# Graph network kernel: products of the first graph layer in the record stage, fixed memory map, graph layers written out from the last node tile

## What is computed

```python
for l in range(3):
    neigh = segment_sum(h[src], dst, n) * inv_deg
    h = h @ Ws_self[l] + neigh @ Ws_neigh[l] + bs[l]
    if l != 2: h = relu(h)
x1 = layernorm(x + h)
# second network, for every edge: e = mlp(edge_attr);
# e_new = mlp([e, mesh_nfeat[src], x1[dst]]) + e
# agg = segment_sum(e_new, dst); n_new = mlp([x1, agg]) + x1
out = layernorm(x1 + n_new)
```

## Time and profile before

| | us |
|---|---|
| runs | 2556.55, 2556.91, 2559.67 (median 2556.91) |
| profiled execution | 2557.4, its span 2555.7 |
| scatters (GpSimd) | from 30.8 to 294 of the span |
| counts (TensorE, VectorE) | from 299.5 to 421.6 |
| P0, S0 | from 431.0 to 492.7, from 497.8 to 550.7 |
| P1, S1 | from 550.9 to 610.5, from 614.0 to 670.1 |
| P2, S2 | from 670.3 to 729.8, from 733.3 to 806.3 |
| P3 | from 806.5 to 868.4 |
| stages c, d | from 876 to the end |

### The profile page before, as it was taken

One profiled execution on the slowest core, in us unless ns is written; L12 is line 12 of the kernel. 1 busy time (PEld: TensorE's weight loads), 2 busy tenths in 40 slices (PEclk: granted clock), 3 DMA queues, 4 the chain that ended last, 5 costly groups with the idle time before them and its releaser, 6 DMA issues. The chain is left out here.

```text
span 2555.7 us, 44732 instructions
## 1 busy us (share of the span) xinstructions
PE 2279.1 (89%) x13410; PEld 1928.7 (75%) x13413; DVE 1410.0 (55%) x3084; ACT 1170.4 (46%) x2117; POOL 1142.9 (45%) x1677
## 2 busy tenths in 40 slices
PE   2991288999988689999999999999999999999888
PEld 1430287777766578888888888888888888888776
DVE  7000297434344256666666666666666666666566
ACT  0210012232321156666666666666666666666521
POOL 4777400202020145555555555555555555555333
PEclk9996699999998889999999999999999999999989
DMA  6221001001012353233233233323232333323121
GB/s 184 78 68 19 14 0 37 11 27 37 1 36 75 101 145 63 60 61 63 59 64 59 63 60 62 62 57 66 57 65 58 62 61 59 64 59 64 30 89 42
DMA packets 76273, 149.57 MB, mean 59 GB/s; under 512 B 14690, under 2 KB 15790, under 8 KB 76220
## 3 DMA queue, kind: packets, MB, share of 16 engines
q0 software_dynamic: 44864, 93.18, 19.0%
q1 hardware_dynamic: 31243, 55.63, 6.6%
q10 hardware_dynamic: 112, 0.11, 0.0%
HBM read 129.12 MB, written 19.46 MB: 58 GB/s over the span
## 5 line engine op out<-in xcount | busy, mean ns | idle before, releaser
L1192 DVE CUSTOM_DVE_ANT_0 c_var_bank<-c_var_bank,c_p,k_floor 128x512 f32<-128x512 f32 x176 | 133.5, 758 | 369.6 <-PE c_var_bank L1349 369.6
L1083 POOL DMA_INDIRECT c_from_src<-s_dst_table,c_at_nodes x176 | 284.0, 1614 | 31.7 <-issue 31.7
L1403 PE MATMUL c_edge_bank<-c_m_hi,c_pt_hi 128*128 128x512 f32 x704 | 291.8, 414 | 0.0
L1404 PE MATMUL c_edge_bank<-c_m_lo,c_pt_hi 128*128 128x512 f32 x704 | 276.7, 393 | 0.0
L1405 PE MATMUL c_edge_bank<-c_m_hi,c_pt_lo 128*128 128x512 f32 x704 | 275.4, 391 | 0.0
L1077 POOL DMA_INDIRECT c_from_src<-s_mesh_table,c_at_nodes x176 | 206.4, 1173 | 150.7 <-POOL c_at_nodes L1073 141.9
L1089 POOL TENSOR_TENSOR c_dev<-c_var,k_half 128x1 f32<-128x1 f32 x176 | 98.1, 557 | 381.8 <-DVE c_var L1179 381.8
L1347 PE MATMUL c_var_bank<-c_m_hi,c_pt_hi 128*128 128x384 f32 x704 | 226.7, 322 | 4.7 <-ACT c_var_bank L1272 4.7
L263 POOL DMA_INDIRECT s_records<-a_stage_rec,a_stage_row x170 | 202.8, 1193 | 56.8 <-issue 48.7
L1347 PE MATMUL c_var_bank<-c_m_hi,c_ht_hi 128*128 128x384 f32 x704 | 226.1, 321 | 0.0
L1298 ACT ACTIVATE c_h<-c_from_src 128x512 f32<-128x512 f32 x176 | 111.2, 632 | 248.5 <-DVE c_from_src L1211 248.5
(11 more groups left out here) (298 smaller groups left out, 6097.9 us busy)
## 6 DMA issues: line engine op xcount, KB each, us to landing
k_w<-in_L_gnn_Ws_self_dram SPq DMA_DIRECT2D x3, 1024.0 KB
k_w<-in_L_gnn_Ws_neigh_dram SPq DMA_DIRECT2D x3, 1024.0 KB
c_from_src<-s_mesh_table,c_at_nodes POOLq DMA_INDIRECT x176
c_from_src<-s_dst_table,c_at_nodes POOLq DMA_INDIRECT x176, 4.7
s_records<-a_stage_rec,a_stage_row POOLq DMA_INDIRECT x170
a_mesh<-in_L_gnn_mesh_nfeat_dram SPq DMA_DIRECT2D x10, 250.0 KB
k_h<-in_x_dram SPq DMA_DIRECT2D x1, 2500.0 KB
s_mesh_table<-a_mesh_out SPq DMA_DIRECT2D x10, 250.0 KB
```

Source lines behind the costliest of these rows:

```text
L1083: pool.indirect_dma_start(from_src[u][:], None, scratch["dst_table"], bass.IndirectOffsetOnAxis(ap=at_nodes[u][:, 1:2], axis=0), compute_o ...
L1192: dve.tensor_tensor_reduce(var1_bank[:], var1_bank[:], p[u % 2][:], 1.0 / D, k["floor"][:, 0:1], ALU.mult, ALU.add, var[u][:, 0:1]).then_i ...
L1403: pe.matmul(edge_bank[:], left[0], m_hi[1][:, c, :], start=False, stop=False, skip_group_check=True)
L1404: pe.matmul(edge_bank[:], left[0], m_lo[1][:, c, :], start=False, stop=False, skip_group_check=True)
```

## The change

1. **P0 moves into stage a.** TensorE makes the products of the first layer after the mesh tiles and ahead of the counts. ScalarE converts the two weight matrices and the first two tiles of `h` ahead of its mesh copies, VectorE writes `w_lo` after its second mesh copy. SyncE issues the bias, the next layer's weights and the next bias ahead of the read-back of the records.
2. **One memory map.** `Region` puts the tensors of both stages at fixed addresses, so that those of P0 outlive stage a. One-hot matrices now lie over the sort's temporaries. No instruction comes of this by itself.
3. **Stage b without loops**, from node tile 9 down to 0, so the S0 pass can begin when only `adj[9]` has been subtracted; each further subtraction is made one tile at a time during S0 (`own_counts`). The test whether the low parts of the counts are needed (`many`) comes at the start of stage b.
4. **TensorE waits for `a_hi`**, and for `a_lo` only inside the branch. The transpose for the next P pass moves from ahead of the last S tile to behind it.
5. **GpSimd splits the second layer's weights at the start of stage b** instead of after P0.
6. **In S2 SyncE loads `x` tile i+2 ahead of its wait for normalised tile i.**

The core of the diff:

```diff
+SORT_AT, TEMP_AT, FOLD_AT, SBUF_END = 87296, 112128, 132864, 229344
@@ phase_a, SyncE
+        sp.dma_start(bias0[:], rows(t["L0_gnn_bs"][0]).broadcast_to([NPB, D])).then_inc(bias_in, 16)
+        sp.wait_ge(w_lo_ok, 2)
+        sp.dma_start(w[0][:], chunked(t["L0_gnn_Ws_self"][1])).then_inc(w_next, 16)
+        sp.dma_start(w[1][:], chunked(t["L0_gnn_Ws_neigh"][1])).then_inc(w_next, 16)
+        sp.wait_ge(self_ok, NB)
+        sp.dma_start(bias0[:], rows(t["L0_gnn_bs"][1]).broadcast_to([NPB, D])).then_inc(bias_next, 16)
@@ phase_a, VectorE, between the second and third mesh copy
+        for i in range(2):
+            dve.wait_ge(w_hi_ok, i + 1)
+            dve.tensor_tensor(w_lo[i][:], w[i][:], w_hi[i][:].bitcast(F32), ALU.subtract).then_inc(w_lo_ok, 1)
@@ phase_a, ScalarE, ahead of the mesh copies
+        act.wait_ge(next_in, 48)
+        for i in range(2):
+            act.activation(w_hi[i][:], w[i][:], ACT.Copy).then_inc(w_hi_ok, 1)
+        for n in range(2):
+            copy_h(n)
@@ phase_a, TensorE, behind the mesh tiles
         pe.wait_ge(row_out_ok, len(vectors))
+        turn_h(0)
+        for n in range(NB):
...
+            for b, j in ((self_bank, 0), (neigh_bank, 1)):
+                last = product(pe, b[u][0:NPB, :], left, (lambda c: w_hi[j][:, c, :], lambda c: w_lo[j][:, c, :]), range(KC))
+            last.then_inc(prod_mm, 1)
+        pe.wait_ge(self_ok, NB)
+        pe.wait_ge(u_lo_ok, NB)
         pe.wait_ge(tables_ok, 1)
@@ phase_b, SyncE
+        for i in range(2):
+            load(i)
+        for i in range(NB):
+            if i + 2 < NB:
+                load(i + 2)
+            sp.wait_ge(h_ok, NB * LAST + i + 1)
+            sp.dma_start(node_rows(scratch["x1"], node(i)), h[:, node(i), :]).then_inc(x1_stored[i % 2], 16)
@@ phase_b, GpSimd
-        for q in range(1, PASSES):
-            pool.wait_ge(w_in, 32 * q)
-            pool.wait_ge(prod_mm, NB * q)
+        for r in range(LAYERS):
+            if r:
+                pool.wait_ge(w_in, 32 * r)
+                pool.wait_ge(prod_mm, NB * r)
@@ phase_b, VectorE, start of the stage
+        own_counts(NB - 1)
+        dve.tensor_copy(degree[:, 0:1], k["degree"][:, 0:1])
+        dve.tensor_tensor(degree[:, 1:], k["degree"][:, 1:], k["degree"][:, 0:NB - 1], ALU.subtract).then_inc(degree_ok, 1)
...
+        own_counts(NB - 2)
+        dve.wait_ge(many_mm, 1)
+        dve.tensor_copy(many_i[:], sum_bank[0][0:1, 0:2]).then_inc(many_read, 1)
...
+        for q in range(LAYERS):
+            rest(q, 0)
+            for i in range(NB):
+                if q == 0 and node(i) >= 3:
+                    own_counts(node(i) - 2)
+                if i + 1 < NB:
+                    rest(q, i + 1)
+                else:
+                    low(q, 0)
+                mix(q, i)
+                if q == LAST and i % 2:
+                    normalise(i - 1)
+            multiply(q)
@@ phase_b, TensorE
+        def add_up(q, i, inexact):
+            g, u = NB * q + i, i % 2
+            pe.wait_ge(a_hi_ok, g + 1)
+            need(pe, mixed_ok, g - 1)
...
+                if s == 0:
+                    with pe.If(inexact > 0):
+                        pe.wait_ge(a_lo_ok, g + 1)
```

More of the change, by code:

```diff
@@ new lines, in rest, with mix @@
+        def rest(q, i):
+            g, u = NB * q + i, i % 2
+            dve.wait_ge(a_hi_ok, g + 1)
+            need(dve, sum_mm, g - 1)
+            dve.tensor_tensor(a_lo[u][:], k["adj"][0:NPB, node(i), :], a_hi[u][:].bitcast(F32),
+                              ALU.subtract).then_inc(a_lo_ok, 1)
+        def mix(q, i):
+            g, u, n = NB * q + i, i % 2, node(i)
+            dve.wait_ge(sum_mm, g + 1)
+            need(dve, h_ok, g - 1)
+            dve.scalar_tensor_tensor(out=mixed[u][:], in0=sum_bank[u][0:NPB, :], scalar=inv_degree[:, n:n + 1],
+                                     in1=h[:, n, :], op0=ALU.mult, op1=ALU.add).then_inc(mixed_ok, 1)
@@ new lines, in normalise @@
+        def normalise(first):
+            pair = (first, first + 1)
+            for i in pair:
+                dve.wait_ge(x_in[i % 2], (i // 2) * 16 + 16)
+                dve.wait_ge(mixed_ok, NB * LAST + i + 1)
+                dve.tensor_tensor(mixed[i % 2][:], mixed[i % 2][:], x[i % 2][:], ALU.add).then_inc(res_ok, 1)
+            for i in pair:
+                dve.wait_ge(res_ok, i + 1)
+                dve.bn_stats(stats[i % 2][:], mixed[i % 2][:]).then_inc(stats_ok, 1)
+            for i in pair:
+                dve.wait_ge(stats_ok, i + 1)
+                dve.sem_inc(tick, 1)
+                dve.bn_aggr(moments[i % 2][:], stats[i % 2][:]).then_inc(moments_ok, 1)
+            for i in pair:
+                dve.wait_ge(moments_ok, i + 1)
+                dve.tensor_scalar(dev[i % 2][:, 0:1], moments[i % 2][:, 1:2], EPS, None, ALU.add).then_inc(var_ok, 1)
+            for i in pair:
+                dve.wait_ge(dev_ok, i + 1)
+                dve.tensor_scalar(h[:, node(i), :], mixed[i % 2][:], moments[i % 2][:, 0:1], dev[i % 2][:, 1:2],
+                                  ALU.subtract, ALU.mult).then_inc(h_ok, 1)
@@ new lines, in multiply @@
+        def multiply(r, i):
+            g, u = NB * r + i, i % 2
+            if i + 1 < NB:
+                turn(r, i + 1)
+            pe.wait_ge(ht_lo_ok, g + 1)
+            if i == 0:
+                pe.wait_ge(w_split, r + 1)
+            need(pe, self_ok, g - 1)
+            need(pe, u_lo_ok, g - 1)
+            left = (lambda c: ht_hi[u][:, c, 0:NPB], lambda c: ht_lo[u][:, c, 0:NPB])
+            for b, j in ((self_bank, 0), (neigh_bank, 1)):
+                last = product(pe, b[u][0:NPB, :], left, (lambda c: w_hi[j][:, c, :], lambda c: w_lo[j][:, c, :]), range(KC))
+            last.then_inc(prod_mm, 1)
@@ new lines, in _ @@
+        pe.wait_ge(many_ok, 2)
+        pe.matmul(sum_bank[0][0:1, 0:2], many[:, 0:1], ones[:], start=True, stop=True).then_inc(many_mm, 1)
+        pe.wait_ge(many_read, 1)
+        inexact = pe.value_load(many_i[0:1, 0:1], min_val=0, max_val=P)
+        for q in range(LAYERS):
+            if q:
+                pe.wait_ge(u_lo_ok, NB * q)
+            for i in range(NB):
+                add_up(q, i, inexact)
+            turn(q, 0)
+            for i in range(NB):
+                multiply(q, i)
```

494 lines of the change are left out of this document (224 added, 270 removed).

## The result

Four executions of the changed kernel took 2471.5, 2475.9, 2477.0 and 2477.5 us, median **2476.5**; the kernel before had a median of 2556.7 beside them. The ratio is 0.968, its 95% interval 0.9665 to 0.9694. The forecast was 2461, its range ended at 2470. The direction and some 80 of the 96 us came true; the end of the range did not hold.

The account below looks back on a forecast made before the run. Scatters bound stage a, TensorE the P passes but not the S passes. Gains of 66.0 (to P1's start), 10.3 (S1) and 20.7 (S2, P3), less 0.5 for scatters, make 96.5: 2461 us, range 2451 to 2470.

Parts of the forecast that it names:

- P0 under the scatters: Stage a: P0 ends near 268, hidden by 24 us of slack; scatters lose 0.5 us, bounds 0 and 13.
- every VectorE operation pushes a scatter: Rival, stage a: each of P0's 35 VectorE operations delays a scatter by its own length, 25 us; 2486, chance 0.04.
- S0's start, 435.1: Start of stage b: S0 begins at 435.1 after VectorE and GpSimd exclude each other; bounds 428 and 437.
- GpSimd's subtraction has gone first ... so tile 8's subtraction ends at 433.95: Start of stage b: GpSimd's subtraction runs 428.8 to 433.2, then VectorE's for tile 8, ahead of line 888, ends at 433.95.
- The bound of 437: Start of stage b: the latest start allowed for S0, against 435.1 expected.
- S0, P1, S1: Stage b: S0 takes 47.8, P1 starts at 484.9 (66.0 gained), S1 takes 49.5 instead of 59.8 (10.3 gained).
- S2 and P3: End of stage b: P3's second product starts at E + 63.6 instead of E + 84.9; 20.7 gained after 0.6 for clock.
- The transfers set 10.3: S2: two loads and two stores per pair keep the queue full, so second adds come 10.3 us apart.
- old rhythm: Rival, S2: the chain store, load, add, normalise stays at 15 us, 19 less gained; 2480, chance 0.08.
- Stages c and d ... are not changed; I carry them over: Behind stage b: stages c and d come behind barriers and keep their times.
- what straight code costs to fetch in stage b: Rival "slower than before": once-fetched straight code costs each of 936 matmuls time; 2639 at 0.19 us more each, chance 0.01.

Follow-up runs that it names:

- e_test_first: Against the changed kernel, VectorE copies the test's result ahead of the subtraction of tile 8's counts instead of behind it; median 2472.0 us, 3.7 less.
- e_split_late: Against the changed kernel, GpSimd's split of the layer-2 weights waits until the test's result has been copied; median 2470.0 us, 5.6 less.
- u_wait_a_lo: Against the changed kernel, TensorE waits again for `a_lo` ahead of every tile of the three S passes; median 2488.1 us, 12.5 more.
- the second profile: The changed kernel run and profiled once more, nothing edited; median of five executions 2475.6 us, the profiled one 2475.7.

## Right or wrong, step by step

The mechanisms of the gain were right: P0 hidden under the scatters, `a_lo` off TensorE's path in S1. What failed are three terms of the sum, each by 4 to 5.5 us: who has the port at S0's start, what sets the rhythm of S2, and stages c and d carried over as they were.

- **P0 under the scatters: right but for its price.** Mesh tiles ended at 206.5 and 205.5 (205.9 said), P0 at 270.6 and 269.3 (268), slack 24 (24). The cost was put at 0.5, bounds 0 and 13. The scatters took 2.4 and 1.5 more in the two profiles; the counts ended at 422.4 and 423.2 where 421.6 + 0.5 = 422.1 was said. What failed is the choice between the bounds: mean and median of the earlier trace rows differ by 3 ns and no operation with two SBUF inputs of this size stood beside a scatter there. The rival "every VectorE operation pushes a scatter" was wrong for the 33 that read the accumulation memory and right in kind for the other two, which pushed the scatters by 1.7 to 2.7 us in all where their length was 4.5.
- **S0's start, 435.1: wrong by 4.1** (17.6 after the counts' end instead of 435.1 - 421.6 = 13.5). The exclusion was right, and so was line 882 waiting. The step that failed is "GpSimd's subtraction has gone first ... so tile 8's subtraction ends at 433.95": it let VectorE have the port after GpSimd's first subtraction, but GpSimd's second had already started. `e_test_first` and `e_split_late` show both halves. The bound of 437 was too near as well. The trace of the kernel before had shown the pair back to back, with a first subtraction that ended at 503.56 and this one behind it:

```profile
503.52 4.62 POOL L682 TENSOR_TENSOR b_w_lo<-k_w,b_w_hi 128x2048 fp32r<-128x2048 f32 x1
```

- **S0, P1, S1: right.** S0 took 47.2 and 48.0 (47.8); P1 began at 489.8 (484.9), all of it the later start; from P1's end to P2's start 50.0 (49.5). `u_wait_a_lo` bears out that the wait for `a_lo` mattered: 5.5 of the 9.7 won.
- **S2 and P3: the mechanism wrong, the size off by 4.1.** "The transfers set 10.3": they did not. 11.0 came from the chain store, load, landing on SyncE's queue, the mechanism of the rival "old rhythm", whose 15 was too long. The first second-add came when said (E + 17.2, E being P2's end); P3's second product started at E + 66.8 instead of E + 63.6, 3.2 later. The clock in its gap was taken as 0.6 and cost 1.6 in the second profile, 2.6 in the first.
- **"Stages c and d ... are not changed; I carry them over": wrong by 5.5.** Their code is not changed, its place is: 3.3 us. The rest, some 2, is the clock after the last pauses, and that part is chance: this stretch took 146.2 and 147.5 us in the two profiles of the kernel before and 143.1 and 148.5 in those of the changed one. The prediction had weighed what straight code costs to fetch in stage b, and not what it does to a loop behind it.

The second profile has a span of 2473.9 where 2555.7 - 96.5 = 2459.2 was said, 14.7 more. The sum is: counts 1.1, S0's start 4.1, S0 to P1's start -0.8, S1 0.5, P2 0.2, S2 and P3 4.1, stages c and d 5.5. That is 14.7. Of the large terms, S0's start, the gap in P3 and the 3.3 of the edge stage each have an experiment that takes them away, and the scatters one that makes their term larger. Open is what decides the clock behind a pause of 3.3 us: nothing in these kernels' traces tells one case from the other.

## What to carry to other kernels

When two engines exclude each other, go on to the next instruction in each queue: the one issued first gets the port (0.11 us decided here), and what a third engine waits for should stand ahead of anything that can be shut out. A rhythm bound by transfers is shown only by transfers without pauses in that very order; first look whether a load stands in a queue behind a store that waits for what the load feeds. And when code ahead of a long loop grows or shrinks, the loop is part of the change: look at the instruction queues' packets in the profile, and move the loop by an instruction or a few if it is fetched in every turn.

## What had not been expected of the hardware

- Six VectorE instructions of 0.06 us ahead of a loop of twenty turns cost 62 us; one made it 3.3 faster; 64 left it as fast as one. The signs in the profile beside the time were 122 against 27 packets of instructions, and 19 pauses of VectorE, 85.1 us in all, that ended on nothing the profile shows.
- A scatter issued during a VectorE subtraction of 2.3 us with both inputs in SBUF lasted until some 1.0 to 1.1 us after its end: 1.9 to 3.2 us instead of 1.19, six times in six and in both profiles of the changed kernel.
- A VectorE `tensor_scalar` of 125 x 10 elements took 4.47 us, until GpSimd's subtraction ended (alone, in the kernel before, 0.17); one of 128 x 1 that started just behind GpSimd's second (433.86) and, in `e_test_first`, a copy from the accumulation memory took 0.14 and 0.15.
- The same pause of 3.3 us left the clock at its upper level in one execution and not in another of the same kernel.
